# Row gathers of an edge attention, counted tile by tile instead of pair by pair

## The reference, cut to what matters

```python
M = Bc * Nc                                   # 8192 nodes
h = (x_flat @ W_gat).reshape(M, HEADS, NUM_EXPERTS)
src = jnp.concatenate([edge_index[0], loops]); dst = jnp.concatenate([edge_index[1], loops])
e = leaky_relu(a_src[src] + a_dst[dst]);  e_max = segment_max(e, dst, num_segments=M)
ee = jnp.exp(e - e_max[dst]);             denom = segment_sum(ee, dst, num_segments=M)
agg = segment_sum(h[src] * (ee / denom[dst])[:, :, None], dst, num_segments=M) + b_gat
...                                           # layernorm, mean over heads, top 2 of 4 experts
```

## Time and profile before

| what | value |
|---|---|
| median of 3 runs | 2807.73 us (2801.46 to 2817.0) |
| the profiled execution's own time | 2809.34 us |
| its span, first to last instruction | 2807.6 us |
| PE busy | 2248.0 us (80%) |
| DVE busy | 1778.6 us (63%) |
| ACT busy | 1369.1 us (49%) |
| POOL busy | 1306.4 us (47%) |
| gathers of line 82 | 178 in phase A, 184 in phase C |

### The profile page before, as it was taken

One profiled execution on the slowest core, in us unless ns is written; L12 is line 12 of the kernel. 1 busy time (PEld: TensorE's weight loads), 2 busy tenths in 40 slices (PEclk: granted clock), 3 DMA queues, 4 the chain that ended last, 5 costly groups with the idle time before them and its releaser, 6 DMA issues. The chain is left out here.

```text
span 2807.6 us, 41748 instructions
## 1 busy us (share of the span) xinstructions
PE 2248.0 (80%) x12080; PEld 1666.7 (59%) x12080; DVE 1778.6 (63%) x4734; ACT 1369.1 (49%) x3028; POOL 1306.4 (47%) x1219
## 2 busy tenths in 40 slices
PE   4989898999999897888506356589999989999990
PEld 2544545465555554655305245488888879888880
DVE  5989989767788575333576853775464584756212
ACT  3554647474755554555414134365555644444540
POOL 1011100100010666567756677326636747767776
PEclk9989999998999998999757678699999998999995
DMA  4010100000010214222231132245455545565762
GB/s 153 1 39 1 32 16 17 16 17 28 5 32 6 51 27 126 81 78 76 54 121 54 35 97 72 70 115 164 122 116 153 147 113 153 141 157 147 183 156 76
DMA packets 278379, 227.90 MB, mean 81 GB/s; under 512 B 85933, under 2 KB 230303, under 8 KB 277234
## 3 DMA queue, kind: packets, MB, share of 16 engines
q1 hardware_dynamic: 243346, 178.97, 21.8%
q0 software_dynamic: 34784, 46.03, 8.7%
HBM read 162.95 MB, written 63.18 MB: 81 GB/s over the span
## 5 line engine op out<-in xcount | busy, mean ns | idle before, releaser
L986 POOL TENSOR_TENSOR a_rstd<-a_var,minus_half 128x4 f32<-128x4 f32 x64 | 98.2, 1534 | 829.4 <-DVE a_var L1540 822.0
L2177 POOL DMA_INDIRECT c_slots<-sent,c_tokens_of_slots x340 | 352.6, 1037 | 203.5 <-PE bank L2348 106.6
L1645 DVE TENSOR_TENSOR room<-room 128x768 f32<-128x768 f32 (+2 forms) x312 | 369.6, 1208 | 31.1 <-ACT room L1382 23.3
L2442 ACT ACTIVATE weights_f<-bank,c_expert_b 128x256 f32<-128x256 f32 x680 | 276.9, 471 | 199.5 <-PE bank L2223 198.7
L2223 PE MATMUL bank<-c_experts_w,weights_f 128*128 x2720 | 347.6, 283 | 18.8 <-ACT weights_f L2442 12.3
L2223 PEld LDWEIGHTS bank<-c_experts_w,weights_f 128*128 128x128 f32 x2720 | 338.9, 199 | 30.1 <-issue 26.0
L2223 PE MATMUL bank<-c_slots_t,c_expert_w 128*128 128x256 f32 x1360 | 342.5, 397 | 17.5 <-ACT weights_f L2442 7.8
L2223 PEld LDWEIGHTS bank<-c_slots_t,c_expert_w 128*128 128x128 f32 x1360 | 255.8, 198 | 54.9 <-issue 19.9
L1016 PE MATMUL bank<-a_h1p,weights_a 128*128 128x512 f32 x544 | 246.9, 605 | 2.3 <-ACT a_dist_exp L1359 2.3
L2639 DVE TENSOR_TENSOR c_made<-bank,c_expert_b 128x256 f32<-128x256 f32 x170 | 72.1, 424 | 268.6 <-PE bank L2223 243.9
L82 POOL DMA_INDIRECT got_room<-table_dram,own_rows x184 | 192.4, 1046 | 75.6 <-issue 75.6
(11 more groups left out here) (532 smaller groups left out, 4548.7 us busy)
## 6 DMA issues: line engine op xcount, KB each, us to landing
c_expert_w<-in_weights_c SPq DMA_DIRECT2D x170, 256.0 KB
made<-c_made SPq DMA_DIRECT2D x170, 128.0 KB
results_dram<-a_results SPq DMA_DIRECT2D x64, 256.0 KB, 2.2
room<-results_dram SPq DMA_DIRECT2D x16, 1024.0 KB, 7.6
c_expert_b<-in_f_b SPq DMA_DIRECT2D x170, 64.0 KB
room<-in_adj SPq DMA_DIRECT2D x32, 256.0 KB, 5.7
sent<-c_rows_to_send SPq DMA_DIRECT2D x32, 256.0 KB, 3.6
c_slots<-sent,c_tokens_of_slots POOLq DMA_INDIRECT x340
```

Of the source, the lines that this page charges most:

```text
L986: rstd.did(g_.tensor_tensor(st.rstd[:, :], st.var[:, :], env.minus_half[:, 0:GT], ALU.pow), what, k)
L1645: v.tensor_tensor((dv[:, :, 0, :], other(dv))[j], sv[:, :, 0, :], other(sv), (ALU.min, ALU.max)[j]).then_inc(sort_step, 1)
L2177: pool.indirect_dma_start(out=XS[p.r % S_BUFS][:, j, :], out_offset=None, in_=env.sent_dram[p.q], in_offset=bass.IndirectOffsetOnAxis(ap=T ...
L2442: go(H[p.m % 2][:, c, :], U[c // 2][:, (c % 2) * SLOT:(c % 2 + 1) * SLOT], func, bias=bias).then_inc(hidden, 1)
```

## The change

Three things change together.

`pair_rows` becomes `tile_rows`: each tile loads its own count and tests it by itself. A new table `LIKELY` has 32 numbers from 12 down to 2, and `LEAST` is two less (at least 1). Tile t of a half fetches `LEAST[t]` slots without a test, then one slot for each of four tests, then four slots on a fifth test, then all up to 23 on a sixth. `count_due` follows, and `pair_slots` becomes `tile_slots`. A task `rows` is now one tile; there are still 32 in each half.

The orders are made with another duration for the gathers: `1.3 * LIKELY[k] + 0.3` us for tile k, in both phases. `PREFER_A` stays.

`PREFER_C` has new numbers throughout, and `SHARED_AFTER` changes from `(0, 0, 6, 13, 19, 31, 40, 80)` to `(0, 0, 6, 11, 21, 31, 36, 88)`.

```diff
-SLOT_CUTS = (0, 2, 3, 4, 5, 6, 7, 8, 9, 10, 12, 14, 18, CAP)
-PIECE_AT = (0, 2, 13)
-PIECES_OF_PAIR = len(PIECE_AT) - 1
+LIKELY = (12, 10, 9, 9, 8) + 4 * (7,) + 4 * (6,) + 5 * (5,) + 7 * (4,) + 4 * (3,) + 3 * (2,)
+LEAST = tuple(max(n - 2, 1) for n in LIKELY)
+SINGLES, FEW = 4, 8
+PIECES_OF_PAIR = AT_TILES
...
-def pair_rows(pool, env, room, pair, piece, landed):
+def tile_rows(pool, env, room, t, landed):
...
-    n = pool.value_load(env.pair_slots[0:1, pair:pair + 1], min_val=0, max_val=CAP)
+    n = pool.value_load(env.tile_slots[0:1, t:t + 1], min_val=0, max_val=CAP)
...
     def fetch(a, z):
-        for t in (2 * pair, 2 * pair + 1):
-            for j in range(a, z):
-                gather_rows(pool, env, room[:, t % AT_TILES, j, :], env.own_rows[:, t, ROW + j:ROW + j + 1].bitcast(U32), landed)
+        for j in range(a, z):
+            gather_rows(pool, env, room[:, t % AT_TILES, j, :], env.own_rows[:, t, ROW + j:ROW + j + 1].bitcast(U32), landed)
...
-    cuts = list(zip(SLOT_CUTS, SLOT_CUTS[1:]))[PIECE_AT[piece]:PIECE_AT[piece + 1]]
-    if piece == 0:
-        fetch(*cuts.pop(0))
-    fetch_from(cuts)
+    least = LEAST[t % HALF]
+    cuts = [least + k for k in range(SINGLES + 1)] + [least + FEW, CAP]
+    fetch(0, least)
+    fetch_from(list(zip(cuts, cuts[1:])))
...
+    for t in range(0, NT):
+        if t % HALF == 0 or LEAST[t % HALF] != LEAST[t % HALF - 1]:
+            run = len([n for n in LEAST if n == LEAST[t % HALF]])
+            ins = v.memset(L.least[:, t:t + run], float(LEAST[t % HALF]))
+    link(ins)
+    link(v.tensor_tensor(L.over, env.tile_f[:, :], L.least, ALU.subtract))
...
+def rows_long(k):
+    return [(POOL, 1.3 * LIKELY[k] + 0.3)]
...
-                    pair_rows(pool, env, R.rows[b % len(R.rows)], b, piece, rows_in[b % len(R.rows)])
+                    tile_rows(pool, env, R.rows[b % len(R.rows)], k, rows_in[b % len(R.rows)])
...
-        pairs = most.rearrange("p (i u) -> p i u", u=2)
-        link(v.tensor_tensor(env.pair_f[:, now], pairs[:, :, 0], pairs[:, :, 1], ALU.max))
...
-SHARED_AFTER = (0, 0, 6, 13, 19, 31, 40, 80)
+SHARED_AFTER = (0, 0, 6, 11, 21, 31, 36, 88)
...
-                    pair_rows(pool, env, R.rows[b % 2], HALF // AT_TILES + b, piece, edge_rows_in[b % 2])
+                    tile_rows(pool, env, R.rows[b % 2], HALF + k, edge_rows_in[b % 2])
```

More of the change, by code:

```diff
@@ L140, in edge_logits @@
     link(v.tensor_scalar(pen, wanted, float(NODES * ROW_STEP), -BIG, ALU.is_ge, ALU.mult))
-    due = dve.value_load(env.rows_due[half][0:1, u, b // len(R.rows):b // len(R.rows) + 1], min_val=16 * AT_TILES * SLOT_CUTS[1], max_val=16 * CAP * HALF // 2)
+    due = dve.value_load(env.rows_due[half][0:1, u, b // len(R.rows):b // len(R.rows) + 1], min_val=16 * AT_TILES * min(LEAST), max_val=16 * CAP * HALF // 2)
     dve.wait_ge(rows_landed[u], due)
@@ L182, in __init__ @@
         self.last_acc = self.take([NT, 16])
-        self.due_f, self.due_step = self.take([1, NT // 2])[:, 0, :], self.take([1, NT // 2])[:, 0, :]
+        self.least, self.over, self.due_f, self.due_step = (self.take([1, NT])[:, 0, :] for n in range(4))
         self.due_sum = [self.take([u, AT_BATCHES // u]) for u in EDGE_ROOMS]
@@ L192, in count_due @@
     v = nc.vector
[L193 to L199, removed]
+    for t in range(0, NT):
[4 more added lines that the diff above has]
+    link(v.tensor_tensor(L.over, env.tile_f[:, :], L.least, ALU.subtract))
+    link(v.tensor_scalar(L.due_f, L.over, 0.0, float(SINGLES), ALU.max, ALU.min))
+    link(v.tensor_scalar(L.due_step, L.over, float(SINGLES), float(FEW - SINGLES), ALU.is_gt, ALU.mult))
+    link(v.tensor_tensor(L.due_f, L.due_f, L.due_step, ALU.add))
+    link(v.tensor_tensor(L.due_f, L.due_f, L.least, ALU.add))
+    link(v.tensor_scalar(L.due_step, L.least, -1.0, float(CAP - FEW), ALU.mult, ALU.add))
+    link(v.scalar_tensor_tensor(L.due_step, L.over, float(FEW), L.due_step, ALU.is_gt, ALU.mult))
+    link(v.tensor_tensor(L.due_f, L.due_f, L.due_step, ALU.add))
+    by_tile = L.due_f.rearrange("p (i u) -> p i u", u=AT_TILES)
+    link(v.tensor_tensor(L.due_step[:, 0:NT // AT_TILES], by_tile[:, :, 0], by_tile[:, :, 1], ALU.add))
+    link(v.tensor_scalar(L.due_step[:, 0:NT // AT_TILES], L.due_step[:, 0:NT // AT_TILES], 16.0, None, ALU.mult))
     for h, rooms in enumerate(EDGE_ROOMS):
@@ L528 @@
     "save": [(SP, 2.5)], "first": [(POOL, 6.6)], "ends": [(PE, 0.5)], "lists": [(SP, 0.6)], "keep": [(SP, 0.6)], "fetch": [(SP, 0.6)], "last": [(SP, 0.6)],
-    "clear": [(DVE, 8.0)], "begin": [(DVE, 3.5), (ACTE, 0.7), (DVE, 3.5)], "rows": [(POOL, 8.5)], "edge": [(DVE, 3.2)], "fall": [(ACTE, 0.45)], "total": [(DVE, 4.6)], "xin": [(SP, 0.6)],
+    "clear": [(DVE, 8.0)], "begin": [(DVE, 3.5), (ACTE, 0.7), (DVE, 3.5)], "edge": [(DVE, 3.2)], "fall": [(ACTE, 0.45)], "total": [(DVE, 4.6)], "xin": [(SP, 0.6)],
     "gates": [(POOL, 0.5), (DVE, 20.0), (ACTE, 0.3), (DVE, 13.0)], "most": [(POOL, 2.0)],
@@ L643, in work_a @@
                    "v1": CHUNKS1 * GROUPS, "v2": EXPERTS1 * GROUPS, "res": EXPERTS1 * GROUPS, "own": owns, "last": 1, "clear": 1, "begin": HALVES, "rows": AT_BATCHES * PIECES_OF_PAIR, "edge": AT_BATCHES, "fall": AT_BATCHES, "total": AT_BATCHES, "gates": 1, "xin": XINS})
-    long = lambda n, k: sort_long(units[k]) if n == "sort" else [(DVE, INDEX[k][1])] if n == "index" else LONG_A[n]
+    long = lambda n, k: sort_long(units[k]) if n == "sort" else [(DVE, INDEX[k][1])] if n == "index" else rows_long(k) if n == "rows" else LONG_A[n]
     in_turn = {"y": N0, "weigh": N0, "comb": N0}
@@ L1829, in index_steps @@
     for h in range(HALVES):
-        tiles, now = slice(h * HALF, (h + 1) * HALF), slice(h * HALF // 2, (h + 1) * HALF // 2)
+        tiles = slice(h * HALF, (h + 1) * HALF)
         dve.wait_ge(maxdeg_done, h + 1)
@@ L1834, in index_steps @@
         link(v.tensor_scalar(env.tile_rounds[:, tiles], env.rounds_f[:, tiles], 1.0, None, ALU.add))
-        pairs = most.rearrange("p (i u) -> p i u", u=2)
-        link(v.tensor_tensor(env.pair_f[:, now], pairs[:, :, 0], pairs[:, :, 1], ALU.max))
-        link(v.tensor_scalar(env.pair_f[:, now], env.pair_f[:, now], float(CAP), None, ALU.min))
-        link(v.tensor_copy(env.pair_slots[:, now], env.pair_f[:, now]))
+        link(v.tensor_scalar(env.tile_f[:, tiles], most, float(CAP), None, ALU.min))
+        link(v.tensor_copy(env.tile_slots[:, tiles], env.tile_f[:, tiles]))
         yield f"rounds_{h}"
@@ L1864 @@
 LONG = {
-    "rows": [(POOL, 7.5)], "edge": [(DVE, 3.9), (ACTE, 0.4), (DVE, 4.1)], "late": [(POOL, 0.3), (DVE, 19.0), (ACTE, 0.3), (DVE, 13.0)],
+    "edge": [(DVE, 3.9), (ACTE, 0.4), (DVE, 4.1)], "late": [(POOL, 0.3), (DVE, 19.0), (ACTE, 0.3), (DVE, 13.0)],
     "load2": [(SP, 2.0)], "sum": [(DVE, 2.25)], "lift": [(DVE, 2.7), (POOL, 3.2)], "lift_end": [(DVE, 0.3), (ACTE, 3.9)], "climb": [(ACTE, 3.9)], "enter_end": [(DVE, 2.5)],
@@ L1880 @@
 PREFER_C = {
[L1881 to L1888, removed]
@@ L1889 @@
-    "soften": (401.0, 180.0), "store": (-5.0, -440.0), "sum": (-336.0, 44.0), "take": (118.0, 26.0), "xt": (-12.0, 223.0)}
-SHARED_AFTER = (0, 0, 6, 13, 19, 31, 40, 80)
+    "adj": (1507.0, 1405.0), "agg": (575.0, -1044.0), "back": (-297.0, 2379.0), "blend": (-286.0, 1810.0), "blend_end": (-419.0, 3070.0),
+    "climb": (-2806.0, -211.0), "compare": (2974.0, 736.0), "conv": (-87.0, -684.0), "ease": (1659.0, -860.0), "ease_end": (539.0, -106.0),
+    "edge": (896.0, 1384.0), "enter_end": (-2769.0, 744.0), "experts": (-522.0, 309.0), "f2_score": (5184.0, 1572.0), "f2_xt": (1046.0, -636.0),
@@ new lines @@
+    "f3_score": (1781.0, 349.0), "f3_xt": (203.0, 1052.0), "fetch": (697.0, -2143.0), "flip": (1909.0, -468.0), "g3_xt": (-548.0, -90.0),
+    "gather": (-2336.0, -434.0), "gather_last": (-2605.0, -1031.0), "late": (-1994.0, 172.0), "leave": (-3698.0, -1702.0), "lift": (1810.0, 599.0),
+    "lift_end": (1535.0, -2352.0), "list": (-425.0, -1152.0), "load2": (-1279.0, -2541.0), "load3": (3529.0, -2883.0), "lower": (-500.0, -153.0),
+    "mark": (1036.0, 1311.0), "mask": (-4031.0, -47.0), "mix": (4455.0, -1537.0), "project": (754.0, 3428.0), "pt": (1575.0, -1047.0),
@@ L1893, in mark_list @@
+    "pull": (-1137.0, -111.0), "raise": (138.0, 1296.0), "route": (823.0, -1138.0), "rows": (-1449.0, -1764.0), "save": (428.0, -1041.0),
+    "settle": (2172.0, -2733.0), "settle_end": (580.0, 543.0), "soften": (-6024.0, -3437.0), "store": (1409.0, -16.0), "sum": (-1407.0, -3214.0),
+    "take": (4591.0, -691.0), "xt": (1164.0, -717.0)}
+SHARED_AFTER = (0, 0, 6, 11, 21, 31, 36, 88)
 def mark_list():
@@ L1980, in work_c @@
     totals.update({n: len(passes) for n in ("raise", "lower", "take")})
-    return {(n, k): Task(LONG[n], needs[n](k), LANDS.get(n, 0.0), (n, k - 1) if k else None) for n in needs for k in range(totals[n])}
+    return {(n, k): Task(rows_long(k) if n == "rows" else LONG[n], needs[n](k), LANDS.get(n, 0.0), (n, k - 1) if k else None) for n in needs for k in range(totals[n])}
 def phase_c(nc, env):
```

(2 more changed lines are left out.)

## The result

The changed kernel takes 2952.17 us (median of 4 runs, 2946.42 to 2953.73), the kernel before 2809.66 us beside it: ratio 1.0504, 95% interval 1.0486 to 1.0523. That is slower by 143 us, as forecast in direction. The forecast size was 107 us (2916): 2952 lies inside the given range of 2848 to 2985, but above the forecast's own 2890 to 2945. By the number alone the rival of compounding queues, 2958, is nearer; which mechanism it was has to come from the timelines and the experiments.

What follows compares the result with a forecast made beforehand. PE was taken to set the pace except around the two edge attentions, where POOL's gathers and ACT's exponentials hold it up; 2809 + 54 + 60 - 7 = 2916 us, given range 2848 to 2985, the forecast's own 2890 to 2945.

Steps and rivals of the forecast that it cites:

- Direction of the tiles: In the gathers' table: counts rise over the tiles while LIKELY falls from 12 to 2.
- Count and step of the gathers: POOL's row gathers: 238 and 239 instead of 178 and 184, each still a step of about 1.3 us.
- Phase A, +54: First half's gathers: 60 more, with waits for rooms, end phase A at 1478 against 1422.4 us; bounds +46 and +96.
- Phase C, +60 for the gathers: Second half's gathers: 55 more cost 74 us, partly filling POOL's idle time; +60 us taken, between +36 and +74.
- The new lists of phase C, -7: PE's order in phase C: two routed passes run before turn 4's shared passes, -7 us; bounds -45 and +25.
- Tests, 0: Tests on POOL before gathers: 105 per half instead of 73, taken to cost 0 us.
- The new order pays for it: Rival: phase C's refilled lists take back the 114 us, so not slower, about 2805 us; chance 0.05.
- Only one stretch pays: Rival: early waits are filled in phase C, or lists hide one stretch: 2863 us; chance 0.10.
- Queues compound: Rival: on POOL, own gathers stand between rows, or POWs behind the last pair's gathers: 2958 to 2990 us; chance 0.12.
- The table fits: Rival: counts fall as the table does, so 346 gathers, 16 fewer, -21 us, 2788 us; chance 0.02.

Runs made afterwards that it cites:

- E1: The changed kernel with LIKELY turned round, rising over the tiles as the counts do; LEAST and list durations follow: 2780.08 us, ratio 0.9905.
- E2: The changed kernel with only LEAST turned round (171 and 175 gathers), all lists of work kept: 2863.58 us, ratio 1.0206.
- E3: The kernel before, its gathers kept, with falling durations, new offsets and new shared passes in its lists: 2874.96 us, ratio 1.0252.
- E4: The changed kernel, its gathers kept, with all lists of work made as in the kernel before: 2914.08 us, ratio 1.0389.
- E8: The kernel before with only the gathers' durations in the lists changed to the falling ones, both phases: 2940.72 us, ratio 1.0475.
- E10: The changed kernel with the old offsets and old shared passes of phase C, table left falling: 3016.64 us, ratio 1.0751.
- E7: E1 with one slot fetched untested and each further slot behind its own test: 2777.66 us, ratio 0.989.

## Why the prediction was right, and where its size was off

**Direction of the tiles: right.** E1 turns a loss of 5% into a gain of 1% with that one line.

**Count and step of the gathers: right.** 477 gathers, medians of 0.998 and 1.008 us, gaps of 0.30.

**Phase A, +54: mis-sized, measured +66.6.** The chain was the right one up to the gates: rooms, last pair, gates. (The prediction's own ends, 1478 and 1422.4, give +55.6; it wrote +54.) Waits for rooms were taken as 10 us; the changed kernel's wait for line 83 is 95.0 us, less 238 gaps of 0.30 and the start of 7.7, 16 us:

```profile
POOL room L83 <- issue: 95.0, 238, 7.7
ACT room L1466 <- DVE room L150: 71.0, 3, 48.7
```

So the gathers end at 1434.8, not 1429. And the end is set by the own rows, which the prediction had arriving "in time": it took 42 us for them and nothing for their landing, where rows 3 have 43.9 from the first start to the last end. The gates are over at 1474.8, DVE then waits 6.4 us for the own rows (the row of line 226 above) and begins at 1481.2, not 1472. DVE is through at 1487.4, and phase C begins 2.1 us later, because POOL closes the phase with a DRAIN after its gathers (start 1481.4, 7.9 us); in the kernel before it ended together with DVE, at 1422.7. So here POOL's own queue ends the phase: in the changed kernel and in E2, E3, E4, E8 and E10 phase C begins 55.3 to 55.8 us after the last row gather starts. E4, with the old lists, has +51.5 for the gathers alone.

**Phase C, +60 for the gathers: right, with the old lists.** E4 measures +57.4 at the last gather's start and 1436.5 - 1384.7 = +51.8 on the whole phase. In the changed kernel that start comes 87.7 us later, beyond the +74 that the prediction had as its upper bound; what is above E4 came with the lists.

**The new lists of phase C, -7: the step that failed.** "I take only the -7": on top of E4 the changed kernel's phase C is longer by 1460.9 - 1436.5 = +24 us, at the edge of the bound of +25. The prediction asked what `SHARED_AFTER` and the offsets could move on PE, and left out what the falling durations do in the same lists, and what the lists put on POOL, which sets the pace there. E8 and E3 show the parts with the old gathers: the durations +131 us over both phases, the offsets and shared passes -60 to -66. The two passes moved ahead are there (32 of the 99 more matmuls are the second halves of two routed passes), and behind the last gather the time is 5.9 us shorter than in E4, close to the 7 forecast, though no more than E1 and E7 differ by. But the stretch before it is 30.3 us longer than in E4. POOL's rows from the begin of phase C to the end of its last row gather (busy + idle just before, us; count):

| POOL | before | E4 | E3 | changed |
|---|---|---|---|---|
| row gathers | 192.4 + 75.6 (184) | 247.0 + 87.0 (239) | 192.8 + 74.1 (184) | 249.3 + 87.6 (239) |
| `c_slots`, gathers for routed passes | 24.6 + 7.1 (24) | 24.7 + 7.1 (24) | 32.5 + 9.5 (32) | 32.8 + 9.5 (32) |
| POWs of the layernorms | 18.1 + 20.2 (10) | 18.4 + 11.2 (10) | 20.1 + 59.4 (12) | 20.1 + 26.5 (12) |
| stretch, with 2.0 of memsets | 340.0 | 397.4 | 390.4 | 427.7 |

From E4 to the changed kernel the row gathers add 3 us. Eight more gathers for routed passes add 10.5, and the POWs 17.0: two more of them, and longer waits for the DVE work in front. E8 tells the two apart: with the falling durations alone it has 24 of the `c_slots` gathers, as before, but its POWs wait 51.4 us. So the offsets and shared passes bring the gathers, and the durations the waits.

With the +12.6 of phase A, the 31 of the lists (24 + 7) and the -8 of the gathers in phase C make 2809 + 54 + 60 - 7 into the 2952 measured.

**Tests, 0: right, and now shown.** E7 has 156 tests more than E1. At the 108 ns that the Trainium skill gives for a compare-and-branch (Advanced Engine Details and Errata, Control Flow Timing) they would be an estimated 17 us, if the engine saw them. The traces differ from it: the records above last 34 ns at the median, 5 us for 156, and POOL's idle time before the gathers is the same to 0.1 us, so these tests cost nothing that the run shows.

**The rivals.** "The new order pays for it" was half true: offsets and shared passes do take back 60 to 66 us, but from a loss that came with the same lists. "Only one stretch pays" did not come: both pay. "Queues compound" came near in time, 2958 against 2952, but not by its mechanism: the own rows stayed behind the gathers, no POW stands behind the last pair's (DVE's longest wait for one is 5.9 us), and only two gathers for routed passes do. In E4 a POW does stand there, DVE waits 44.3 us for it, and phase C is no longer than forecast. "The table fits" is excluded by the counts.

What stays open: which entries of the offsets take back the 60 to 66 us, and why the old offsets put so few matmuls ahead of the barrier under falling durations (789 in E8 and E10 alike, so not because of the gathers). No run parts `PREFER_C` from `SHARED_AFTER`.

## What to carry to other kernels

A table of expected sizes is an input twice, to the code and to whatever plans the order; check its direction against a trace (the first wait, the groups between waits) before anything else. Offsets that are set together with wrong durations can hide part of the error: here they took back 60 to 66 of 131 us, and made no difference once the durations were right. A wait that ends earlier is worth only what the engine that sets the pace behind it gains by it: count the work that is done ahead of the wait, and see which list fixes that count. And when work is moved ahead on the engine that idles, look at what it brings to the engine that sets the pace: here the passes moved ahead for PE brought gathers for POOL.

## What the runs showed of the hardware

An indirect gather in which no node has an edge left costs POOL the same as a full one. The last two tiles of the second half hold counts of 11 and 13 and fetch 23 slots each. So the 12 gathers issued from 1871.5 to 1886.6 us find nothing to fetch, and the 10 from 1890 to 1903 us, slots 2 to 11 of the last tile, are fuller; by the seeded edges the first of them has a row for each of the 128 nodes. The software queue of the changed kernel in the two stretches (packets, MB, share of 16 engines):

```profile
q0 software_dynamic: 384, 0.01, 1.9%
```

```profile
q0 software_dynamic: 320, 0.09, 6.6%
```

Both are 32 packets a gather; the first carry next to nothing. POOL's timeline has one row of each, an empty one and that full one:

```profile
1875.51 1.00 POOL L83 DMA_INDIRECT got_room<-table_dram,own_rows  x1 [0.30 <-issue]
...
1889.93 1.01 POOL L83 DMA_INDIRECT got_room<-table_dram,own_rows  x1 [0.30 <-issue]
```

1.00 and 1.01 us, with the same gap: what a gather costs POOL here does not depend on what it moves.

A compare-and-branch on POOL's queue is a record of 34 ns (346 of them in E7), and between gathers it adds nothing to the gap of 0.30 us.

The DRAIN that closes phase A on POOL takes 7.2 to 7.9 us in the runs looked at (7.4 before, 7.9 in the changed kernel), and it can end a phase when POOL's gathers come last.
